# Decay attention: three waits for one count of folded weights become five waits, and the folding is split over the first steps

## The chip, the cores and the metric

The kernel runs on one core of one Trainium2 chip. The metric is the device time of one execution in microseconds, the median over several runs. A profile is one further execution, recorded by the hardware profiler. TensorE is called PE below, its weight loads PEld, VectorE DVE, ScalarE ACT, GpSimd POOL and SyncE SP.

## The reference

The program is a small language model tower on 128 x 128 tokens with 64 channels: an embedding with gates, an attention, a block with mixture of experts, a decay attention and a selected MLP. The change is in the fourth. Cut to it:

```python
low = conv(x, conv_w) + conv_b                     # 5 causal taps over the sequence
hid = layernorm(low + sqrt_beta**2 * (x - low) + x, ln_w, ln_b)
q, k, v = proj(q_w, q_b), proj(k_w, k_b), proj(v_w, v_b)      # 8 heads of 8
scores = q @ k.T / sqrt(8)
p_ = softmax(where(mask, scores, -1e32)) * mask
dist = sqrt(clip((p_.sum(-1) - cumsum(p_)) * pos, 0))
total_effect = clip(exp(-softplus(gammas) * dist), 1e-5, 1e5)
p = softmax(where(mask, scores * total_effect, -1e32)); p[first row] = 0
out = (p @ v) @ out_w.T + out_b
h = h + out        # x is layernorm(h), h includes the experts' output
```

## The kernel before, in words

The tower is five phases, one after another, each a block with one instruction list per engine, written by hand. A phase ends with a barrier over all engines, after which its semaphores are cleared. The residual H (128 partitions x 128 blocks x 64) stays in SBUF all the time. The phase of experts leaves its rows in DRAM (`back_rows`), and `slot` says where each token's row is.

`phase_decay_attention` works on 32 groups of 4 blocks. A group has 4 steps, one for each pair of heads, so 128 steps, numbered K. Each engine runs one loop over K from -24 to 136, with m = K // 4 and j = K % 4. In step K an engine does what is due for pair K, K-1, K-2 and K-3, and at fixed j something for a group ahead: on POOL four gathers (`d_moe`, one in each step, L1463) for group m+6, the join into H (L1476) for m+5 at j = 2, the mean and the centring (`d_mean`, `d_hc`, L1489, L1491) for m+3 at j = 0, the output bias (`d_cb` added to H, L1497) for m+2 at j = 1, and at j = 2 `d_hn` (L1504) for m+2 and `d_xn` (L1510) for m+3. DVE sums H for the mean (L1942) for m+4 at j = 3 and the squares (`d_ss`, the spread, L1890 and L1895) at j = 1. PE turns `d_xn` and `d_hn` (L1578) at j = 3, filters with the taps (`d_conv`, L1603) and projects with `d_wqk` and `d_wv` at j = 0 to 2 and makes the first scores (L1532) of a pair with `d_hide` as mask. So steps -24 to -1 are a ramp in which one group after another goes through gather, join, layer norm, turn, filter, second norm, turn and projection; scores, exponentials, a scan along the keys on DVE (L1901), the decay (`d_decay`, with the positions `d_posg`, L1452 to L1457) on POOL and the weighting follow from K = 0. Order on an engine is fixed; all that isn't due waits behind what is.

Ahead of the loops the weights are loaded by SP (18 loads, L1440) and folded by DVE: the blend with `sqrt_beta` goes into the taps (`d_conv`, `d_convb`), the layer norm's scale and shift into the projections (`d_wqk`, `d_wv`, `d_bqk`, cut into three bf16 parts in `d_bqk_s`), the value bias through the output weights into `d_cb`, `softplus(gammas)` squared into `d_posg`, and the mask into bf16 `d_hide`. A helper `link` makes each DVE instruction wait for the one before. Constants are set by memsets. Fourteen of these instructions add one to the semaphore `ready`, and POOL, PE, ACT and DVE all wait for 14 ahead of their loops:

```python
READY = 14
pool.wait_ge(ready, READY)        # likewise pe, act and dve
for K in range(FIRST, LAST + 1):
```

## Time and profile before

| | us |
|---|---|
| runs | 2621.09, 2600.0, 2622.05; median 2621.09 |
| profiled execution, its time | 2639.77 |
| profiled execution, its span | 2638.0 |
| busy in the span: PE, DVE, ACT, POOL | 2189.6, 1804.3, 1295.3, 1675.9 |
| mean granted TensorE clock | 0.831 of full speed |
| decay attention, from its first load to the end of the last group | about 1263 to 2450 |

The span is from the first to the last instruction of the profiled execution; about 1.8 us of its time lie outside. A busy share tells how much an engine had to do, and the idle time ahead of a group of instructions, with what released it, tells who waited for whom. Times of single instructions are read in the timeline. The granted clock is 0.50 or 1.00 at any moment (1.2 or 2.4 GHz), so a mean between them tells how long it was at each.

### The profile page before, as it was taken

How to read it: one execution, taken by the hardware profiler on the slowest of the kernel's cores; microseconds unless marked ns; L12 is line 12 of the kernel's file. 1: busy time of each engine (PE TensorE's matmuls, PEld its weight loads, DVE VectorE, ACT ScalarE, POOL GpSimd, SP SyncE). 2: the span in 40 equal slices, each digit the busy share in tenths (PEclk: the TensorE clock that was granted, in tenths of full speed). 3: DMA queues.
4: the chain of work that ended last, by engine and by line, in shares of the span. 5: the costliest groups of instructions: out<-in, count | busy, mean ns of one | idle time of the engine just before them, and what ended most of it. 6: DMA issues, size and time to landing. Idle time of an engine off the chain costs nothing. (4 is left out here: it accounts for less than half of the span.)

```text
span 2638.0 us, 56358 instructions
## 1 busy us (share of the span) xinstructions
PE 2189.6 (83%) x20636; PEld 1661.1 (63%) x20636; DVE 1804.3 (68%) x3575; ACT 1295.3 (49%) x2690; POOL 1675.9 (64%) x1809
## 2 busy tenths in 40 slices
PE   6999859999970589998199889999889988998485
PEld 5988736777750455554067677777667776766374
DVE  4599636777749945554368878888888878876524
ACT  1244315666640234444056666666666666665342
POOL 6366113444420765553389999999999999885261
PEclk9999758999985589999578877788888778875587
DMA  2111000000014045668100000000000000000003
GB/s 47 24 38 40 7 8 14 26 22 26 22 33 2 23 103 145 148 145 120 39 7 6 5 6 6 5 6 5 6 6 6 5 5 5 2 1 1 4 1 64
DMA packets 111567, 78.16 MB, mean 30 GB/s; under 512 B 71533, under 2 KB 92269, under 8 KB 111312
## 3 DMA queue, kind: packets, MB, share of 16 engines
q1 hardware_dynamic: 95248, 48.59, 8.2%
q0 software_dynamic: 16064, 26.17, 5.6%
q8 instruction: 161, 2.64, 0.4%
q14 instruction: 94, 0.77, 0.1%
HBM read 56.03 MB, written 18.68 MB: 28 GB/s over the span
## 5 line engine op out<-in xcount | busy, mean ns | idle before, releaser
L1901 DVE TENSOR_TENSOR_SCAN d_later<-d_cont,d_ex 128x768 f32<-128x768 f32 x128 | 283.3, 2213 | 27.1 <-ACT d_ex L1714 26.8
L1684 ACT ACTIVATE d_pT<-d_T 128x384 f32<-128x384 f32 x256 | 125.5, 490 | 295.7 <-PE d_T L1545 295.4
L1545 PE MATMUL d_T<-ident,d_p 128*128 128x128 f32 x768 | 169.3, 339 | 84.3 <-POOL d_p L1470 76.3
L1452 POOL TENSOR_TENSOR d_decay<-d_later,d_posg 128x768 f32<-128x768 f32 x128 | 232.8, 1819 | 9.5 <-DVE d_later L1901 9.5
L1456 POOL TENSOR_TENSOR d_decay<-d_decay,d_rtot 128x512 f32<-128x512 f32 x128 | 179.0, 1399 | 18.9 <-POOL d_decay L1452 0.9
L1463 POOL DMA_INDIRECT d_moe<-back_rows,slot x128 | 130.8, 1022 | 83.5 <-DVE d_mean L1852 60.1
L1532 PEld LDWEIGHTS d_S<-d_kT,d_qT 16*128 16x128 f32 x2048 | 149.9, 220 | 51.5 <-issue 51.5
L1469 POOL TENSOR_TENSOR d_p<-d_p,d_mx 128x512 f32<-128x512 f32 x128 | 162.7, 1271 | 28.7 <-DVE d_mx L1884 26.9
L1532 PEld LDWEIGHTS d_R<-d_kT,d_qT 16*128 16x128 f32 x2048 | 148.5, 218 | 51.2 <-issue 51.2
L1878 DVE SCALAR_TENSOR_TENSOR d_p<-d_decay,d_R 128x768 f32<-128x768 f32 x128 | 121.5, 950 | 85.6 <-PE d_R L1532 54.3
L1532 PE MATMUL d_S<-d_kT,d_qT 16*128 16x128 f32 (+1 forms) x2048 | 169.1, 313 | 0.0
L1532 PE MATMUL d_R<-d_kT,d_qT 16*128 16x128 f32 (+1 forms) x2048 | 167.5, 310 | 0.0
L1545 PEld LDWEIGHTS d_T<-ident,d_p 128*128 128x128 f32 x768 | 95.2, 164 | 112.2 <-POOL d_p L1470 86.2
L223 POOL DMA_INDIRECT rows<-in_table,idx x128 | 122.0, 953 | 35.6 <-issue 31.3
L1720 ACT ACTIVATE d_decay<-d_decay 128x768 f32<-128x768 f32 x128 | 107.3, 838 | 74.9 <-POOL d_decay L1457 74.9
L1457 POOL TENSOR_TENSOR d_decay<-d_decay,d_rtot 128x256 f32<-128x256 f32 x128 | 141.8, 1108 | 0.0
L1322 DVE TENSOR_TENSOR e_cont<-e_h,e_upto 128x512 f32<-128x512 f32 x91 | 62.9, 692 | 107.4 <-ACT e_upto L1199 107.4
L1603 PE MATMUL d_X<-d_conv,d_xT 128*128 128x128 f32 x640 | 119.9, 370 | 1.5 <-ACT d_xT L1773 1.5
L1603 PEld LDWEIGHTS d_X<-d_conv,d_xT 128*128 128x128 f32 x640 | 118.3, 286 | 2.6 <-ACT d_xT L1773 2.6
L1714 ACT ACTIVATE d_ex<-d_ex 128x768 f32<-128x768 f32 x128 | 107.7, 841 | 9.1 <-DVE d_ex L1870 7.8
L1722 ACT ACTIVATE d_decay<-d_decay 128x768 f32<-128x768 f32 x128 | 107.9, 843 | 4.1
L1724 ACT ACTIVATE d_decay<-d_decay 128x768 f32<-128x768 f32 x128 | 107.9, 843 | 4.1
(400 smaller groups left out, 6118.4 us busy)
## 6 DMA issues: line engine op xcount, KB each, us to landing
e_upto<-in_pair_w SPq DMA_DIRECT2D x55, 288.0 KB
e_cont<-in_pair_w SPq DMA_DIRECT2D x36, 288.0 KB
sent_rows<-moe_rows SPq DMA_DIRECT2D x32, 256.0 KB, 2.8
back_rows<-e_ys SPq DMA_DIRECT2D x91, 64.0 KB
out_h<-g_Y SPq DMA_DIRECT2D x8, 512.0 KB, 4.0
rows<-in_table,idx POOLq DMA_INDIRECT x128
d_moe<-back_rows,slot POOLq DMA_INDIRECT x128, 2.5
e_tie<-sent_rows,e_token POOLq DMA_INDIRECT x62
```

What stands on the lines that cost most here:

```text
L223: pool.indirect_dma_start(rows[u][:, b, :], None, dram["table"], bass.IndirectOffsetOnAxis(ap=idx[u][:, b:b + 1], axis=0))\
L1452: pool.tensor_tensor(decay[d][:], later[u][:, 0:2 * SEG].rearrange("p (e s) -> p e s", e=2), posg[:, h:h + 2, :], ALU.mult).then_inc(U["pl ...
L1456: pool.tensor_tensor(long(decay[d]), long(decay[d]), wide(rtot[u], 1, P), ALU.mult)
L1457: pool.tensor_tensor(short(decay[d]), short(decay[d]), wide(rtot[u], 0, HALF), ALU.mult)\
L1463: pool.indirect_dma_start(moe[n % KEEP_M][:, j, :], None, back_rows, bass.IndirectOffsetOnAxis(ap=slot[:, b:b + 1], axis=0))\
L1469: pool.tensor_tensor(long(p2[w]), long(p2[w]), wide(mx2[u], 1, P), ALU.subtract)
L1532: last = nc.tensor.matmul(bank[:, e, cols], qT[s][r, c, (2 * g + S) * P:(2 * g + S + 1) * P], kT[s][r, c, keys], start=False, stop=(g == 1 ...
L1545: last = nc.tensor.transpose(bT[:, t * P:(t + 1) * P], p2[K % KEEP_P][:, e, t * P:(t + 1) * P], ident[:])
L1603: last = nc.tensor.matmul(X1[:, g * P:(g + 1) * P], xT[:, g, tap:tap + P], conv[:, tap, :], start=(tap == 0), stop=(tap == TAPS - 1))
L1684: nc.scalar.activation(pT[w % KEEP_T][:], bT[:, 0:SEG], ACT.Exp).then_inc(U["pT_kept"], 1)
L1878: nc.vector.scalar_tensor_tensor(p2[w][:], decay[d][:], 1e-5, bR[:, :, 0:SEG], ALU.max, ALU.mult).then_inc(U["weighed"], 1)
L1901: nc.vector.tensor_tensor_scan(later[u][:, 1:1 + 2 * SEG], cont[:], ex[u][:].rearrange("p e s -> p (e s)"), 0.0, ALU.mult, ALU.add)\
```

## The change

The count of 14 stays, but its increments come in another order and each engine waits only for the part that it needs next. `READY` becomes five numbers. POOL waits for nothing ahead of its loop; PE, ACT and DVE wait for 8 (four memsets, the bf16 identity, the ones, the taps, the filter's bias). The projections' fold, with `d_cb`, becomes `fold_projections`, called on DVE at the top of step -11; the positions' and the mask's fold becomes `fold_places`, called at the top of step -6. Waits for 11, 12, 13 and 14 stand at the first use of the parts on PE and POOL. The memsets and the cast of the identity move ahead of DVE's wait for the loads. What is computed is the same.

```diff
-        READY = 14
+        CONV_READY, PROJECT_READY, BIAS_READY, PLACE_READY, SCORE_READY = 8, 11, 12, 13, 14
...
             def _(pool):
-                pool.wait_ge(ready, READY)
...
                         pool.wait_ge(U["scanned"], K)
+                        if K == 1:
+                            pool.wait_ge(ready, PLACE_READY)
...
+                            if n == 0:
+                                pool.wait_ge(ready, BIAS_READY)
                             pool.tensor_tensor(hs, hs, cb[:, None, :].to_broadcast([P, GB, D]), ALU.add)\
...
-                pe.wait_ge(ready, READY)
+                pe.wait_ge(ready, CONV_READY)
...
+                        if K + 1 == 0:
+                            pe.wait_ge(ready, SCORE_READY)
...
+                        if m + 1 == 0:
+                            pe.wait_ge(ready, PROJECT_READY)
...
-                act.wait_ge(ready, READY)
+                act.wait_ge(ready, CONV_READY)
...
             def _(dve):
-                dve.wait_ge(loaded, 16 * LOADS)
...
+                nc.vector.memset(xT[:, :, 0:PADT], 0.0).then_inc(ready, 1)
...
+                dve.wait_ge(loaded, 16 * LOADS)
...
+                link(nc.vector.tensor_tensor(bv[:], X1[:, 0:1], bv[:], ALU.add))
+                nc.vector.tensor_copy(bv_wide[:], bv[:, 0:1].to_broadcast([P, P])).then_inc(carried, 1)
+                dve.wait_ge(ready, CONV_READY)
+
+                def fold_projections():
...
+                def fold_places():
...
                 for K in range(FIRST, LAST + 1):
                     m, j = K // PAIRS, K % PAIRS
+                    if K == -11:
+                        fold_projections()
+                    if K == -6:
+                        fold_places()
```

The two functions hold the removed lines word for word, but that the wait for the second fold on PE now stands ahead of the scaling of `d_wqk`.

The start of POOL's list in this phase, before (d_moe are the gathers, H the residual; a wait's semaphore stands in brackets):

```order
L1442 UNCONDITIONAL_BRANCH [waits barrier_Pool_Activation_PE_DVE_SP_gather]
L1463 DMA d_moe<-back_rows,slot 128x64 [waits d_ready]
L1463 DMA d_moe<-back_rows,slot 128x64 x6
L1476 TENSOR_TENSOR H<-H,d_moe 128x256 [waits d_fetched0]
L1463 DMA d_moe<-back_rows,slot 128x64
```

and of the changed kernel:

```order
L1442 UNCONDITIONAL_BRANCH [waits barrier_Pool_Activation_PE_DVE_SP_gather]
L1464 DMA d_moe<-back_rows,slot 128x64 x7
L1477 TENSOR_TENSOR H<-H,d_moe 128x256 [waits d_fetched0]
L1464 DMA d_moe<-back_rows,slot 128x64
L1464 DMA d_moe<-back_rows,slot 128x64 [waits a_rstd_made0] x3
```

The wait for `d_ready` is gone; the order of the instructions is the same.

DVE's list in the projections' fold, before (d_bqk and d_bqk_s are the query and key bias and its bf16 parts, d_bv the value bias):

```order
L1812 TENSOR_SCALAR d_convb<-d_convb,d_biassum 128x64
L1815 TENSOR_TENSOR d_bqk<-d_X,d_bqk 3x512
L1816 TENSOR_SCALAR d_bqk<-d_bqk 3x256
L1817 CAST d_bqk_h<-d_bqk 3x512
L1818 TENSOR_TENSOR d_bqk_rest<-d_bqk,d_bqk_h 3x512
L1819 CAST d_bqk_m<-d_bqk_rest 3x512
L1820 TENSOR_TENSOR d_bqk_l<-d_bqk_rest,d_bqk_m 3x512
```

and the same place in the changed kernel:

```order
L1831 TENSOR_SCALAR d_convb<-d_convb,d_biassum 128x64
L1834 TENSOR_TENSOR d_bqk<-d_X,d_bqk 3x512
L1835 TENSOR_TENSOR d_bv<-d_X,d_bv 128x1
L1836 COPY d_bv_wide<-d_bv 128x128
L1956 TENSOR_REDUCE d_mean<-H 128x4
L1840 TENSOR_SCALAR d_bqk<-d_bqk 3x256
L1841 CAST d_bqk_h<-d_bqk 3x512
```

The first sum over H (L1956) now stands ahead of the fold, and the twelve instructions from L1840 to L1853 stand ahead of the first spread (L1904).

DVE's list around the first second-norm spread, before:

```order
L1928 TENSOR_TENSOR d_zb<-d_X,d_convb 128x256
L1890 TENSOR_REDUCE d_ss<-d_sq 128x4
L1895 TENSOR_REDUCE d_ss<-d_sq 128x4
L1942 TENSOR_REDUCE d_mean<-H 128x4
L1928 TENSOR_TENSOR d_zb<-d_X,d_convb 128x256
```

and in the changed kernel (d_gam and d_posg are the decay rates and the scaled positions):

```order
L1942 TENSOR_TENSOR d_zb<-d_X,d_convb 128x256
L1904 TENSOR_REDUCE d_ss<-d_sq 128x4
L1909 TENSOR_REDUCE d_ss<-d_sq 128x4
L1858 TENSOR_SCALAR d_gam<-d_gam 128x8
L1859 TENSOR_TENSOR d_gam<-d_gam,d_gab 128x8
L1860 TENSOR_TENSOR d_gam<-d_gam 128x8
L1861 TENSOR_TENSOR d_posg<-d_pos,d_gam 128x3072
L1863 CAST d_hide<-d_hide_f 128x384
L1956 TENSOR_REDUCE d_mean<-H 128x4
L1942 TENSOR_TENSOR d_zb<-d_X,d_convb 128x256
```

The five instructions of the positions and the mask now stand between the two spreads and the sum over H.

## Rows read from the trace of the kernel before

**Rows 1.** Busy time by stage: start:end, length, each engine's busy us, TensorE clock, DMA share, GB/s.
```profile
1263.00:1273.30 10.30, 0.00 (x0) 0.00 (x0) 0.00 (x0) 1.28 (x1) 0.00 (x0) 0.50 0.60 167
1336.00:2256.00 920.00, 833.19 (x9317) 651.92 (x9314) 748.59 (x1307) 577.63 (x1039) 877.75 (x855) 0.82 0.03 5
1336.00:1376.00 40.00, 38.41 (x252) 29.63 (x250) 30.66 (x53) 19.88 (x36) 36.08 (x39) 0.66 0.03 6
1576.00:1616.00 40.00, 37.62 (x398) 29.41 (x398) 31.76 (x57) 23.95 (x43) 38.23 (x40) 0.82 0.03 6
```

**Rows 2.** Waits in 1260 to 1345: us in total, times, longest.
```profile
POOL d_moe L1463 <- DVE d_mean L1852: 60.1, 1, 60.1
```

**Rows 3.** Timeline, first load and first DVE instruction: start, us, engine, line, operation [idle before].
```profile
1263.01 0.35 SPq L1440 DMA_DIRECT2D d_wqk<-in_d_wqk  x1
...
1273.31 0.17 DVE L1794 TENSOR_SCALAR d_gab<-d_gam 128x8 f32<-128x8 f32 x1 [12.94 <-DMA d_diag<-in_ident]
```

**Rows 4.** Timeline of DVE, the folding of the weights.
```profile
1279.12 0.28 DVE L1816 TENSOR_SCALAR d_bqk<-d_bqk 3x256 f32<-3x256 f32 x1
...
1283.59 0.14 DVE L1825 TENSOR_TENSOR d_bv<-d_X,d_bv 128x1 f32<-128x1 f32 x1
...
1283.90 0.48 DVE L1827 TENSOR_SCALAR d_wqk<-d_wqk,d_lnw 128x512 f32<-128x512 f32 x1
...
1285.02 0.16 DVE L1834 TENSOR_SCALAR d_gam<-d_gam 128x8 f32<-128x8 f32 x1
...
1285.61 3.36 DVE L1837 TENSOR_TENSOR d_posg<-d_pos,d_gam 128x3072 f32<-128x3072 f32 x1
...
1293.43 0.06 DVE L1852 MEMSET d_mean<- 128x4 f32 x1
```

**Rows 5.** Timeline of POOL, the ramp.
```profile
1293.80 0.94 POOL L1463 DMA_INDIRECT d_moe<-back_rows,slot  x1 [60.13 <-DVE d_mean L1852]
...
1311.02 0.22 POOL L1489 TENSOR_SCALAR d_mean<-d_mean 128x4 f32<-128x4 f32 x1
...
1314.39 0.73 POOL L1476 TENSOR_TENSOR H<-H,d_moe 128x256 f32<-128x256 f32 x1
1315.07 0.61 POOL L1510 TENSOR_TENSOR d_xn<-d_hc,d_rstd 128x256 f32<-128x256 f32 x1
...
1323.25 0.61 POOL L1504 TENSOR_TENSOR d_hn<-d_zb,d_rstd 128x256 f32<-128x256 f32 x1 [0.37 <-ACT d_rstd L1689]
1323.82 0.61 POOL L1510 TENSOR_TENSOR d_xn<-d_hc,d_rstd 128x256 f32<-128x256 f32 x1
```

**Rows 6.** Timeline of DVE and PE, the ramp.
```profile
1312.49 0.42 DVE L1890 TENSOR_REDUCE d_ss<-d_sq 128x4 f32<-128x256 f32 x1 [8.98 <-ACT d_sq L1706]
...
1322.61 0.41 DVE L1942 TENSOR_REDUCE d_mean<-H 128x4 f32<-128x256 f32 x1
...
1324.49 0.69 PE L1578 MATMUL d_X<-ident,d_xn 128*128 128x128 f32 x2 [3.16 <-POOL d_xn L1510]
```

**Rows 7.** Timeline where POOL starts beside a DVE instruction, and one alone.
```profile
1791.20 1.76 DVE L1901 TENSOR_TENSOR_SCAN d_later<-d_cont,d_ex 128x768 f32<-128x768 f32 x1 [0.29 <-ACT d_ex L1714]
...
1791.37 2.43 POOL L1463 DMA_INDIRECT d_moe<-back_rows,slot  x1 [0.15 <-issue]
...
2461.76 1.22 DVE L2155 SCALAR_TENSOR_TENSOR g_X<-g_sums,H 128x1024 f32<-128x1024 f32 x1
2461.78 1.78 POOL L2034 TENSOR_TENSOR g_xw<-g_X,g_wr 128x256 f32<-128x256 f32 x1
...
2464.90 0.72 POOL L2034 TENSOR_TENSOR g_xw<-g_X,g_wr 128x256 f32<-128x256 f32 x1
```

**Rows 8.** Timeline of POOL, d_decay at the start of three groups.
```profile
1513.23 1.83 POOL L1452 TENSOR_TENSOR d_decay<-d_later,d_posg 128x768 f32<-128x768 f32 x1
...
1548.22 1.83 POOL L1452 TENSOR_TENSOR d_decay<-d_later,d_posg 128x768 f32<-128x768 f32 x1
...
1582.24 1.85 POOL L1452 TENSOR_TENSOR d_decay<-d_later,d_posg 128x768 f32<-128x768 f32 x1
```

More of the change, by code:

```diff
@@ L1791, in link @@
                     dve.wait_ge(chain, steps[0])
+                nc.vector.memset(xT[:, :, 0:PADT], 0.0).then_inc(ready, 1)
+                nc.vector.memset(rstd[:], 0.0).then_inc(ready, 1)
+                nc.vector.memset(rstd2[:], 0.0).then_inc(ready, 1)
+                nc.vector.memset(mean[:], 0.0).then_inc(ready, 1)
+                nc.vector.tensor_copy(ident_b[:], ident[:]).then_inc(ready, 1)
+                nc.vector.memset(ones[:], 1.0).then_inc(ready, 1)
+                for u in range(2):
+                    nc.vector.memset(later[u][:, 0:1], 0.0).then_inc(chain, 1)
+                for u in range(KEEP_V):
+                    nc.vector.memset(v[u][:, :, :, HD:HD + 1], 1.0).then_inc(chain, 1)
+                    nc.vector.memset(v[u][:, :, :, HD + 1:], 0.0).then_inc(chain, 1)
+                steps[0] += 2 + 2 * KEEP_V
+                dve.wait_ge(chain, steps[0])
+                dve.wait_ge(loaded, 16 * LOADS)
                 nc.vector.tensor_scalar(gab[:], gam[:], -1.0, None, ALU.mult).then_inc(softened, 1)
@@ L1842, in _ @@
-                for u in range(2):
-                    nc.vector.memset(later[u][:, 0:1], 0.0).then_inc(chain, 1)
-                for u in range(KEEP_V):
-                    nc.vector.memset(v[u][:, :, :, HD:HD + 1], 1.0).then_inc(chain, 1)
-                    nc.vector.memset(v[u][:, :, :, HD + 1:], 0.0).then_inc(chain, 1)
-                steps[0] += 2 + 2 * KEEP_V
-                dve.wait_ge(chain, steps[0])
-                nc.vector.memset(xT[:, :, 0:PADT], 0.0).then_inc(ready, 1)
-                nc.vector.memset(rstd[:], 0.0).then_inc(ready, 1)
@@ L1851, in _ @@
-                nc.vector.memset(rstd2[:], 0.0).then_inc(ready, 1)
-                nc.vector.memset(mean[:], 0.0).then_inc(ready, 1)
-                dve.wait_ge(ready, READY)
+                dve.wait_ge(ready, CONV_READY)
+                def fold_projections():
+                    link(nc.vector.tensor_scalar(bqk[:, 0:2 * P], bqk[:, 0:2 * P], HD ** -0.5, None, ALU.mult))
+                    link(nc.vector.tensor_copy(bqk_h[:], bqk[:]))
+                    link(nc.vector.tensor_tensor(bqk_rest[:], bqk[:], bqk_h[:], ALU.subtract))
+                    link(nc.vector.tensor_copy(bqk_m[:], bqk_rest[:]))
+                    link(nc.vector.tensor_tensor(bqk_l[:], bqk_rest[:], bqk_m[:], ALU.subtract))
+                    link(nc.vector.tensor_scalar(bias[:], bqk_h[:], ident[0:3, 0:1], None, ALU.mult))
+                    link(nc.vector.scalar_tensor_tensor(bias[:], bqk_m[:], ident[0:3, 1:2], bias[:], ALU.mult, ALU.add))
+                    nc.vector.scalar_tensor_tensor(bias[:], bqk_l[:], ident[0:3, 2:3], bias[:], ALU.mult, ALU.add)\
+                        .then_inc(ready, 1)
+                    dve.wait_ge(folded, 2)
+                    link(nc.vector.tensor_scalar(wqk[:], wqk[:], lnw[:, 0:1], None, ALU.mult))
+                    nc.vector.tensor_scalar(wqk[:, 0:2 * P], wqk[:, 0:2 * P], HD ** -0.5, None, ALU.mult).then_inc(ready, 1)
+                    nc.vector.tensor_scalar(wv[:], wv[:], lnw[:, 0:1], None, ALU.mult).then_inc(ready, 1)
+                    nc.vector.scalar_tensor_tensor(cb[:], bT[:, 0:D], notfirst[:, 0:1], outb[:], ALU.mult, ALU.add)\
+                        .then_inc(ready, 1)
@@ new lines, in fold_places @@
+                def fold_places():
+                    dve.wait_ge(softened, 4)
+                    link(nc.vector.tensor_scalar(gam[:], gam[:], 0.0, None, ALU.max))
+                    link(nc.vector.tensor_tensor(gam[:], gam[:], gab[:], ALU.add))
+                    link(nc.vector.tensor_tensor(gam[:], gam[:], gam[:], ALU.mult))
+                    nc.vector.tensor_tensor(posg[:], pos[:, None, :].to_broadcast([P, NH, SEG]), over(gam[:], SEG), ALU.mult)\
+                        .then_inc(ready, 1)
+                    nc.vector.tensor_copy(hide[:], hide_f[:]).then_inc(ready, 1)
```

24 lines of the change are left out of this document (removed).

## The prediction

> **What bounds the kernel now.** I read the busy time by stage first, then the longest waits around the start of the decay attention, then the timeline of each engine there. The stage has two parts. Once it runs, POOL is its bound: busy 877.75 of 920 us, 95%, where PE has 833.19 and DVE 748.59 [rows 1]. But before it runs there is a long hole: POOL waits 60.1 us, in one piece, for DVE's last memset [rows 2]. The loads of the stage are issued from 1263.01 and DVE's first instruction starts at 1273.31 [rows 3]; DVE then folds weights until 1293.43 [rows 4], and POOL's first gather of the expert rows starts at 1293.80 [rows 5]. Nothing of the stage runs beside this: all engines wait for one count of 14. After it a ramp (gather, join, layer norm, turn, filter, second norm, projection) leads to the first scores, and the POOL-bound flow follows. As each engine goes through its list in order, what the ramp starts earlier ends earlier, unless something new is late in it.
>
> **The wait removed, on POOL.** POOL now waits for nothing of the stage before the first gather. It follows the same barrier as the loads of 1263.01, and 1293.80 came 0.3 us after the memset that released it, so the first gather starts near 1263.3, 30.5 us earlier. Its own work from the first gather to the first mean (d_mean, 1311.02) took 17.2 us [rows 5]: 1280.5. From there to the end of the third join (1314.39 + 0.73) it is 4.1 us: 1284.6.
>
> **The prologue that stays, on DVE.** Memsets and the cast of the identity now stand ahead of the wait for the loads and are hidden by them (10.3 us without DVE work). The chain on the filter taps is unchanged and starts at 1273.31. The instruction at 1279.12 [rows 4] is the first that moves out; the bias and its wide copy come in (about 0.4 us, the distance 1283.59 to 1283.90 and one start more), so DVE enters its loop at about 1279.6. The first sum over H takes 0.4: 1280.0. That is just ahead of POOL's 1280.5, so neither waits long.
>
> **The first part moved, K = -11.** The projection fold stands on DVE between the first sum and the first spread. It is 1279.12 to 1283.59 and 1283.90 to 1285.02 [rows 4], 4.5 + 1.1 = 5.6 us: DVE gets to the spread at 1285.6. The squares for it are there by 1282.0 (the spread followed d_mean by 1312.49 - 1311.02 = 1.5 us [rows 5, 6]), so 3.6 us of waiting are new here. From the spread to a possible start of d_hn or d_xn are the 0.42 of the sum and two small activations, about 1 us (the next time round d_hn at 1323.25 followed 0.64 us behind the start of the instruction after such a spread [rows 5, 6]), so the first d_xn starts at 1286.6 where POOL would be free at 1284.6: 2.0 us of the 30.5 are given back, and the chain at this point runs through the loads, DVE's prologue and this fold. First gain: 1315.07 - 1286.6 = 28.5 us.
>
> **What the overlap costs there.** Before, POOL stood still while DVE folded; now both work. The trace shows what DVE and POOL do to each other: a gather that starts under a scan of DVE takes 2.43 us instead of 0.94, a POOL tensor_tensor under a scalar_tensor_tensor of DVE takes 1.78 instead of 0.72 [rows 5, 7]. Both are DVE instructions with two operands in SBUF. DVE in turn waits for a running POOL instruction. In 1280 to 1285.6 POOL wants to run d_mean 0.22, d_hc (as d_xn) 0.61 and a join 0.73, 1.56 us; and a join stands beside the tap chain (0.73). Bounds: nothing, or 2.3 us. The nearest rows are these collisions, so I take 1.5, plus 0.3 us for the 18 loads, since eight gathers of 32 KB join 1.7 MB there at a DMA share of 0.60 [rows 1] (bounds 0 and 1.6 us, 256 KB at the 167 GB/s shown). POOL's own delay by DVE, up to 0.7 us for each of some 10 gathers and joins, is free as long as it stays under 2 + 1.8 us. Gain at the first d_xn: 28.5 - 1.8 = 26.7 us.
>
> The trace of before has no row in which POOL runs beside a DVE instruction with a single SBUF source. The Trainium skill, page "SBUF — State Buffer", section "SBUF: two separate sides", says that such instructions, in their two-port mode (an fp32 copy is its example), shut GpSimd out too, and that a gather issued by GpSimd then waits for its descriptors. That speaks against this change: eight gathers and more now stand beside tensor_scalars, casts and copies. By it POOL would use up its slack, and the sum would be at the second rival's time; no row here shows it.
>
> **The second part moved, K = -6.** The positions fold (d_gam, then d_posg 3.36 us, then d_hide) stands on DVE after two spreads and ahead of a sum over H. In time of before, d_posg would start 0.59 us (1285.02 to 1285.61 [rows 4]) after 1322.61 [rows 6], at 1323.20. POOL starts d_hn at 1323.25 and d_xn at 1323.82 [rows 5]. d_posg has two SBUF operands like the scan and the instruction of rows 7, so I count that it keeps POOL out for its whole length: whichever comes first, d_xn ends 3.3 us later. And d_xn is what PE waits for: it turns it at 1324.49 [rows 6], and filter, projections and first scores hang on that. The sum over H behind d_posg comes about 4 us later than 1322.61, but POOL asks for it only after this d_xn, two gathers and two copies, which are late by the same 3.3 us: hidden. Bounds 0 and 3.7 us; I take 3.3, from the nearest rows. d_cb, the bias weights and d_hide are done long before POOL, PE or the scores ask for them, at K = -7, -4 and -1; those new waits cost nothing.
>
> **Sum.** 30.5 - 2.0 - 1.8 - 3.3 = 23.4 us, which no later stage gives back by its order, since POOL has the same list. The profiled execution took 2639.77 us (span 2638.0), 18.7 above the median of the runs, 2621.09. Against its own time the sum gives 2616.4; against the median 2597.7.
>
> **Rivals.**
> First: d_posg doesn't hold POOL (no row shows a plain tensor_tensor of this length beside POOL), and the mutual waits are small. Then 26.7 to 28.5 us stay: 2594.4 to 2592.6, just over 1%. For it: POOL runs unhindered beside all DVE instructions that read PSUM. Against: both instructions of rows 7.
>
> Second: the prologue's gathers or their landing become the path. With 15 gathers ahead of the first d_xn, and 10 of them under DVE's work, 0.7 us each (half of the 1.49 of rows 5 and 7) is 7 us: POOL ends the third join at 1291.6, d_xn is 3.2 us later than my 1288.4, and the gain 20 us: 2601. With 1.4 us each it would be 13 us: 2608. Loads that come late through the gathers' share of the queues act in the same direction, one for one.
>
> Third, in the flow: the distance of every fourth d_decay was 35.0 us (1513.23 to 1548.22) and then 34.0 (1548.22 to 1582.24) [rows 8], by how DVE's scans fall against POOL's instructions. A start in another position could hold one of them: half a microsecond in each of the 26 groups that 920 us hold is 13 us, in either direction. I put that in the range.
>
> Fourth, slower: TensorE's clock. In 1336 to 1376 the granted clock was 0.66, PE was busy 38.41 of 40 us and POOL only 36.08; at 0.82 POOL had 38.23 [rows 1]. If the changed start led to the low clock all through the stage, PE would be the bound: 920 x (38.23 / 36.08 - 1) = 55 us more, minus 23 is 32 slower: 2653. It decides where the mean clock of the stage falls to about 0.7, from 0.82. Against: the clock was at 0.50 ahead of this stage before, too [rows 1], and most of POOL's idle time in that window is the ramp itself.
>
> **How the numbers follow.** Forecast 0.49, first rival 0.19, second 0.21, third in its harmful form 0.06, fourth 0.05. The likeliest gives 2597.7 us. The runs of before lie between 2600.0 and 2622.05, so 1% (26 us) is also about what a measurement tells from no change. The lowest end takes the first rival or the useful form of the third, 2597.7 less 24: 2574; the highest leaves a third of the second rival and of the harmful third above it, 2612. Faster by over 1% needs 26.2 us: the first rival, and one part in three of the forecast with the third's useful half, 0.35. Slower by over 1% is the fourth, 0.05. The rest, 0.60, is within 1%.
>
> **What would show it.** Right: a first gather at 1263 to 1264; the first sum over H near 1280; the first spread 5.6 to 7 us behind it with POOL waiting for the reciprocal deviation; a d_hn or d_xn of about 3.9 us beside d_posg; that d_xn 22 to 25 us before its 1323.82; POOL busy 95% after. Wrong: gathers of 1.5 us and more in the prologue, loads that end after 1275, no long d_xn beside d_posg, or an unchanged start of the flow.

## The result, and the profile after

The changed kernel takes 2597.51 us in the median of 20 runs (2580.04 to 2641.18); the kernel before, run beside it, 2620.0 us (2600.0 to 2656.05, 20 runs). The ratio is 0.9914, with a 95% interval of 0.989 to 0.9938: about 22.5 us less, between 16 and 29. The ratios here and below, with their intervals, are taken over the fast runs alone, those within 1.5% of the fastest of the same kernel. The profiled execution has a span of 2600.9 us where the one of before had 2638.0. These two spans differ by 37.1 us, more than the runs do, and the first thing to read is how little of that is the change.

I take the trace apart at two points that every profile of this kernel has: the issue of the decay attention's first load, and the first table load of the last phase (the selected MLP) on ACT. Ahead of the first point the two programs are the same, and behind the second too.

| us | before | changed |
|---|---|---|
| phases ahead, to the first load | 1263.01 | 1242.84 |
| first load to the first scores | 72.56 | 45.43 |
| first scores to the last phase | 1112.73 | 1112.57 |
| last phase | 189.70 | 200.06 |
| span | 2638.0 | 2600.9 |

So 37.1 = 20.2 + 27.1 + 0.2 - 10.4. Only the 27.1 belongs to the change; the 20.2 and the 10.4 are chance, as the experiments below show. All times from here on that are called "after the first load" are counted from the first row of the table.

The busy time by stage of the changed kernel (start:end, length, PE, PEld, DVE, ACT, POOL busy, clock, DMA share, GB/s): the loads, then a 920 us stretch of the flow like that of [rows 1], then the middle of the last phase.

```profile
1242.90:1253.20 10.30, 0.00 (x0) 0.00 (x0) 3.79 (x14) 1.23 (x1) 7.71 (x9) 0.50 0.69 189
1315.70:2235.70 920.00, 834.20 (x9453) 652.94 (x9451) 741.66 (x1311) 583.69 (x1049) 876.26 (x853) 0.82 0.02 5
...
2434.50:2506.50 72.00, 68.92 (x402) 55.50 (x404) 16.36 (x43) 28.31 (x53) 51.85 (x79) 0.70 0.00 1
```

Where [rows 1] had DVE and POOL at 0.00 while the loads ran, they now have 3.79 and 7.71. In the flow nothing changed: POOL 876.26 of 920 against 877.75, clock 0.82. In the last row PE is busy 68.92 of 72 us at a clock of 0.70. The same stretch of the kernel before is this:

```profile
2482.00:2554.00 72.00, 60.69 (x425) 49.08 (x425) 19.39 (x50) 30.01 (x56) 58.84 (x89) 0.83 0.00 1
```

More matmuls (425 against 402) in the same 72 us with less busy time, at 0.83. At 0.70 PE is busy 96% of the stretch, at 0.83 84%: the longer last phase goes with the lower clock.

The longest waits around the start of the phase in the changed kernel (us in total, times, longest; 1240 to 1325):

```profile
POOL d_moe L1464 <- POOLq L91: 31.6, 1, 31.6
...
PE d_X L1581 <- POOL d_xn L1513: 10.7, 2, 7.5
...
DVE d_zb L1942 <- PE d_X L1606: 8.9, 2, 6.3
```

POOL's 60.1 us for the last memset [rows 2] became 31.6, and what releases it is its own queue passing the barrier. Nothing of that wait is left in this phase. Next come waits of 6 to 8 us of PE for POOL and of DVE for PE: the ramp waits for itself now, one engine for the next.

The timeline of the changed kernel in the prologue and ramp, all engines (start, us, engine, line, operation [idle before]):

```profile
1242.84 0.35 SPq L1440 DMA_DIRECT2D d_wqk<-in_d_wqk  x1
...
1243.48 0.94 POOL L1464 DMA_INDIRECT d_moe<-back_rows,slot  x1 [31.62 <-POOLq L91]
...
1254.00 0.17 DVE L1813 TENSOR_SCALAR d_gab<-d_gam 128x8 f32<-128x8 f32 x1 [6.82 <-DMA d_diag<-in_ident]
...
1255.33 1.42 POOL L1464 DMA_INDIRECT d_moe<-back_rows,slot  x1 [0.30 <-issue]
...
1258.01 1.39 POOL L1477 TENSOR_TENSOR H<-H,d_moe 128x256 f32<-128x256 f32 x1
...
1260.41 0.41 DVE L1956 TENSOR_REDUCE d_mean<-H 128x4 f32<-128x256 f32 x1
1260.74 0.27 DVE L1840 TENSOR_SCALAR d_bqk<-d_bqk 3x256 f32<-3x256 f32 x1
...
1261.90 0.37 POOL L1490 TENSOR_SCALAR d_mean<-d_mean 128x4 f32<-128x4 f32 x1
...
1262.66 0.98 DVE L1844 TENSOR_TENSOR d_bqk_l<-d_bqk_rest,d_bqk_m 3x512 bf16<-3x512 f32 x1
...
1267.07 0.40 DVE L1904 TENSOR_REDUCE d_ss<-d_sq 128x4 f32<-128x256 f32 x1
...
1268.03 0.61 POOL L1513 TENSOR_TENSOR d_xn<-d_hc,d_rstd 128x256 f32<-128x256 f32 x1 [1.42 <-ACT d_rstd L1696]
...
1276.01 0.61 POOL L1507 TENSOR_TENSOR d_hn<-d_zb,d_rstd 128x256 f32<-128x256 f32 x1 [0.18 <-ACT d_rstd L1696]
...
1276.10 0.54 DVE L1860 TENSOR_TENSOR d_gam<-d_gam 128x8 f32<-128x8 f32 x1
1276.58 0.61 POOL L1513 TENSOR_TENSOR d_xn<-d_hc,d_rstd 128x256 f32<-128x256 f32 x1
1276.68 3.73 DVE L1861 TENSOR_TENSOR d_posg<-d_pos,d_gam 128x3072 f32<-128x3072 f32 x1
...
1277.34 3.93 POOL L1464 DMA_INDIRECT d_moe<-back_rows,slot  x1
...
1288.25 0.61 POOL L1507 TENSOR_TENSOR d_hn<-d_zb,d_rstd 128x256 f32<-128x256 f32 x1 [0.24 <-ACT d_rstd L1696]
1288.27 1.11 PE L1535 MATMUL d_S<-d_kT,d_qT 16*128 16x128 f32 x16
```

The reader should see four things. The first gather starts 0.64 us after the first load. The first sum over H starts as soon as DVE's prologue ends (1260.41), and the fold between it and the spread (1260.74 to 1267.07) is what POOL waits 1.42 us for in front of the first d_xn. The second d_xn (1276.58) starts 0.10 us ahead of d_posg (1276.68) and takes its normal 0.61; the gather behind it is the one that d_posg holds, 3.93 us instead of 0.99. And the d_hn of the next group (1288.25) has waited 0.24 us for its reciprocal deviation. The timeline of the kernel before, at the same two instructions:

```profile
1335.55 0.61 POOL L1504 TENSOR_TENSOR d_hn<-d_zb,d_rstd 128x256 f32<-128x256 f32 x1 [3.26 <-ACT d_rstd L1689]
1335.57 1.11 PE L1532 MATMUL d_S<-d_kT,d_qT 16*128 16x128 f32 x16
```

It waited 3.26 us. The three microseconds that the gather lost to d_posg were three that POOL would have stood idle a little later.

### The profile page after: what moved, and what is told of

It is laid out like the page before. It is cut to its first block and busy times, and to the rows that moved or that the text cites. A ratio compares the mean times of both kernels' runs of the same rounds, so it can differ in the third digit from the quotient of the medians.

```text
span 2600.9 us, 56361 instructions
## 1 busy us (share of the span) xinstructions
PE 2181.0 (84%) x20636; PEld 1652.0 (64%) x20636; DVE 1799.9 (69%) x3575; ACT 1294.4 (50%) x2690; POOL 1682.9 (65%) x1809
## 5 line engine op out<-in xcount | busy, mean ns | idle before, releaser
L1915 DVE TENSOR_TENSOR_SCAN d_later<-d_cont,d_ex 128x768 f32<-128x768 f32 x128 | 277.1, 2165 | 32.0 <-ACT d_ex L1721 31.8
L1470 POOL TENSOR_TENSOR d_p<-d_p,d_mx 128x512 f32<-128x512 f32 x128 | 158.9, 1242 | 28.7 <-DVE d_mx L1898 26.9
L1464 POOL DMA_INDIRECT d_moe<-back_rows,slot x128 | 141.4, 1105 | 55.0 <-POOLq L91 31.6
L1606 PE MATMUL d_X<-d_conv,d_xT 128*128 128x128 f32 x640 | 113.4, 356 | 1.5 <-ACT d_xT L1780 1.5
L1606 PEld LDWEIGHTS d_X<-d_conv,d_xT 128*128 128x128 f32 x640 | 111.1, 271 | 2.6 <-ACT d_xT L1780 2.6
```

What stands on the lines that cost most here:

```text
L1464: pool.indirect_dma_start(moe[n % KEEP_M][:, j, :], None, back_rows, bass.IndirectOffsetOnAxis(ap=slot[:, b:b + 1], axis=0))\
L1470: pool.tensor_tensor(long(p2[w]), long(p2[w]), wide(mx2[u], 1, P), ALU.subtract)
L1606: last = nc.tensor.matmul(X1[:, g * P:(g + 1) * P], xT[:, g, tap:tap + P], conv[:, tap, :], start=(tap == 0), stop=(tap == TAPS - 1))
L1915: nc.vector.tensor_tensor_scan(later[u][:, 1:1 + 2 * SEG], cont[:], ex[u][:].rearrange("p e s -> p (e s)"), 0.0, ALU.mult, ALU.add)\
```

## The experiments

Theory A is that of the prediction: the gain is the head start of POOL's list minus what ends last in the ramp, each microsecond of the ramp reaches the end of the flow one for one, and d_posg keeps POOL out for its length, so that it costs 3.3 us when it starts ahead of a d_hn or d_xn and nothing when it holds a gather. The rivals are that d_posg doesn't matter, that the loads or the flow's position decide, or that the 22.5 us have more to do with chance than with the ramp; each expectation says which it is about. For each run the places read are the same. Times are after the first load but for the last two columns, the first load itself and the span; the first column is empty where DVE starts on four loads instead of 18.

| us | first DVE work | first d_xn | second d_xn | first scores | scores to last phase | last phase | first load at | span |
|---|---|---|---|---|---|---|---|---|
| before | 10.30 | 52.06 | 60.81 | 72.56 | 1112.73 | 189.70 | 1263.01 | 2638.0 |
| changed | 11.16 | 25.19 | 33.74 | 45.43 | 1112.57 | 200.06 | 1242.84 | 2600.9 |
| changed, again | 10.70 | 24.72 | 33.21 | 44.83 | 1109.10 | 200.03 | 1234.94 | 2588.9 |
| changed, third | 10.76 | 24.70 | 33.10 | 44.70 | 1109.10 | 189.58 | 1223.82 | 2567.2 |
| d_posg first | 11.22 | 25.80 | 37.26 | 49.37 | 1113.01 | 189.61 | 1278.61 | 2630.6 |
| fold one step later | 11.01 | 22.83 | 35.63 | 46.42 | 1111.52 | 189.60 | 1256.16 | 2603.7 |
| gathers wait for loads | 10.30 | 32.95 | 45.14 | 56.21 | 1108.29 | 189.67 | 1231.53 | 2585.7 |
| before, POOL's wait removed | 11.09 | 36.16 | 44.50 | 55.99 | 1112.28 | 189.74 | 1267.59 | 2625.6 |
| d_posg from one source | 11.07 | 24.87 | 33.23 | 44.81 | 1109.07 | 189.62 | 1238.40 | 2581.9 |
| taps first | | 22.50 | 32.83 | 43.81 | 1108.29 | 189.61 | 1237.39 | 2579.1 |
| short ramp | | 19.98 | 30.34 | 41.81 | 1112.31 | 189.62 | 1230.36 | 2574.1 |
| taps first, fold two steps later | | 22.92 | 31.74 | 43.33 | 1109.03 | 189.66 | 1235.98 | 2578.0 |

**The changed kernel again.** No edit.

> The changed kernel once more, unchanged. In its profile the last phase took 200.1 us against 189.7 before, with the same instructions, and PE's granted clock in its middle was 0.71 against 0.83; the phases ahead of the decay attention took 20 us less. Theory A (both are the clock's chance, not the change): the time from the phase's first load to the last phase is again 1158 us within 1, while the last phase and the first part take other values. Theory B (the shifted start puts the last phase into a low clock): the last phase takes 200 us again.

It took 2590.72 us. The ramp repeats within 0.6 us (first scores 44.83). Theory A missed in its number all the same: from the first load to the last phase it was 1153.9 us, not 1158 within 1, since the flow came out 3.5 us shorter. And the last phase was 200.03 again, as theory B has it, so the same program ran a third time:

> The changed kernel a third time, unaltered. Both of its profiles so far show a last phase of 200.0 us where the eight other kernels' profiles show 189.6 to 189.7. If that is tied to this kernel's text, it will be 200.0 again; if it is chance (a state of TensorE's clock in that phase), 189.6 is about as likely. Either way the ramp must repeat: d_xn of the second group near 33.2 to 33.7 us after the phase's first load, first scores near 44.8 to 45.4, last phase's start near 1153.9 or 1158.0 after the first load.

It took 2569.01 us, the ramp repeated again (44.70), and the last phase was 189.58, with PE at the clock of the kernel before in the same stretch of that phase:

```profile
2411.30:2483.30 72.00, 60.81 (x425) 49.22 (x425) 19.32 (x50) 29.91 (x55) 58.80 (x89) 0.83 0.00 1
```

So the long last phase isn't tied to the text of the changed kernel. Three profiles of one program differ by 19.0 us (1242.84 against 1223.82) ahead of the first load, by 3.5 us in the flow, and by 10.5 us in the last phase, and by 0.7 us in the ramp. A single span says little about this change; the ramp shows it to within 0.7 us.

**d_posg in front of d_hn.** The three d_gam instructions move from the positions' fold to the end of the projections' fold, so that d_posg starts right behind the spread.

```diff
-
-                def fold_places():
                     dve.wait_ge(softened, 4)
                     link(nc.vector.tensor_scalar(gam[:], gam[:], 0.0, None, ALU.max))
                     link(nc.vector.tensor_tensor(gam[:], gam[:], gab[:], ALU.add))
                     link(nc.vector.tensor_tensor(gam[:], gam[:], gam[:], ALU.mult))
+
+                def fold_places():
                     nc.vector.tensor_tensor(posg[:], pos[:, None, :].to_broadcast([P, NH, SEG]), over(gam[:], SEG), ALU.mult)\
```

The wait for `softened` moves with them.

> The changed kernel with the three small d_gam instructions moved from step -6 to the end of the projections' fold, so that in step -6 d_posg stands first and can start about 1.4 us earlier, before d_hn and d_xn of POOL. Theory A (d_posg costs nothing in the changed kernel only because it starts 0.1 us behind the second d_xn and then holds up a gather instead, whose delay PE doesn't see): now d_hn or d_xn is held for about 3.3 us, the second d_xn comes 36.5 to 37.5 us after the phase's first load instead of 33.7, the first scores 48 to 49 us instead of 45.4. Theory B (d_posg doesn't hold a POOL tensor_tensor, or the ramp has slack for it): the second d_xn stays at 33.7 or, by the fold's three instructions, within 0.6 us of it, and the first scores at 45.4 to 46.

Measured 2632.37 us in one run, with the phase's first load at 1278.61, the latest of all. The timeline of POOL and DVE there:

```profile
1311.91 3.52 DVE L1861 TENSOR_TENSOR d_posg<-d_pos,d_gam 128x3072 f32<-128x3072 f32 x1
...
1312.55 3.35 POOL L1507 TENSOR_TENSOR d_hn<-d_zb,d_rstd 128x256 f32<-128x256 f32 x1 [0.34 <-ACT d_rstd L1696]
1315.87 0.72 POOL L1513 TENSOR_TENSOR d_xn<-d_hc,d_rstd 128x256 f32<-128x256 f32 x1
```

d_hn took 3.35 us instead of 0.61 and ended 0.47 us behind d_posg. The second d_xn is at 37.26 instead of 33.1 to 33.7 and the first scores at 49.37 instead of 44.7 to 45.4, 3.9 to 4.7 us later and beyond the 48 to 49 of theory A. Part of that isn't the collision: the first d_xn is already 0.6 to 1.1 us late, with the three d_gam instructions now in the fold ahead of it. From the first d_xn to the second it is 11.5 us instead of 8.4 to 8.6, about 3 us, near the 3.3 of the prediction. In the changed kernel d_posg started 0.10 us behind the start of the second d_xn, in its two repeats 0.10 and 0.67 us. That d_posg doesn't hold POOL (the first rival) is refuted.

**d_posg from one source.** Eight tensor_scalars, one for each head, in the place of the one tensor_tensor.

```diff
-                    nc.vector.tensor_tensor(posg[:], pos[:, None, :].to_broadcast([P, NH, SEG]), over(gam[:], SEG), ALU.mult)\
+                    for g in range(NH - 1):
+                        nc.vector.tensor_scalar(posg[:, g, :], pos[:], gam[:, g:g + 1], None, ALU.mult).then_inc(chain, 1)
...
+                    nc.vector.tensor_scalar(posg[:, NH - 1, :], pos[:], gam[:, NH - 1:NH], None, ALU.mult).then_inc(ready, 1)
```

> The changed kernel with d_posg made by eight tensor_scalar instructions of 128 x 384 (one SBUF source and one scalar per partition, so one operand stream) instead of one tensor_tensor with two. Theory A (only DVE instructions with two SBUF operands keep POOL out): POOL's gather behind the second d_xn takes its 0.99 us instead of 3.93. Theory B (fp32 instructions with one SBUF source keep it out too, one instruction at a time): the gather starts in a gap between two of them or waits for one, and takes 1.0 to 1.6 us; POOL instructions behind it are lengthened by up to 0.4 us each. In both the fold is some 0.3 us longer or shorter, and the first scores stay at 44.8 to 45.4.

Measured 2583.66 us in one run. Timeline of DVE and POOL:

```profile
1272.30 2.69 DVE L1862 TENSOR_SCALAR d_posg<-d_pos,d_gam 128x384 f32<-128x384 f32 x7
...
1272.39 0.99 POOL L1464 DMA_INDIRECT d_moe<-back_rows,slot  x1
1273.68 1.00 POOL L1464 DMA_INDIRECT d_moe<-back_rows,slot  x1 [0.30 <-issue]
...
1276.23 0.23 POOL L1490 TENSOR_SCALAR d_mean<-d_mean 128x4 f32<-128x4 f32 x1 [0.64 <-DVE d_mean L1959]
```

Neither gather is held (0.99 and 1.00 us), which was the number of theory A. But POOL's next two instructions are, by a little, which was theory B (timeline of POOL):

```profile
1274.69 0.55 POOL L1483 COPY d_hTr<-d_hT 128x256 f32<-128x256 f32 x1
1275.20 0.40 POOL L1484 COPY d_hTr<-d_hT 128x128 f32<-128x128 f32 x1
```

Beside no tensor_scalar, in the changed kernel, they take 0.40 and 0.28 us. And the edit changed two things at once, the number of SBUF operands and the length of each instruction, 0.40 us in the place of 3.36: what starts beside so short a one can be held only for its rest. So this run doesn't show that it is the two operands that hold POOL. Other rows show that one is enough, as here in the timeline of DVE and POOL of the next experiment:

```profile
1256.96 0.47 DVE L1851 TENSOR_SCALAR d_wqk<-d_wqk,d_lnw 128x512 f32<-128x512 f32 x1
...
1257.09 0.92 POOL L1478 TENSOR_TENSOR H<-H,d_moe 128x256 f32<-128x256 f32 x1
```

The join that starts 0.13 us behind this tensor_scalar takes 0.92 us instead of 0.73. A d_hc that starts 0.14 us into the cast d_bqk_m takes 0.74 to 0.75 instead of 0.61 in five profiles. Sums are the exception: no join beside the spread (d_ss) takes more than 0.74.

For two operands, the Trainium skill, page "SBUF — State Buffer", section "SBUF: two separate sides", says that a DVE instruction with two SBUF inputs holds the pair of ports that it shares with GpSimd against a GpSimd instruction that reads SBUF; the traces here agree (3.35 us for d_hn beside d_posg), with gathers held too. The first scores are at 44.81, where two of the three profiles of the changed kernel have 44.70 and 44.83: a gather freed there is worth nothing, since POOL then stands idle 2.21 us ahead of its next d_hn.

**Gathers wait for the loads.** POOL waits for the 18 loads ahead of its loop, and DVE's prologue and fold stay as changed.

```diff
             def _(pool):
+                pool.wait_ge(loaded, 16 * LOADS)
                 for K in range(FIRST, LAST + 1):
```

> The changed kernel with POOL waiting for the 18 loads ahead of its first gather. Theory A (the loads end 0.86 us later than before because eight gathers share the DMA queues with them, and POOL's 15 gathers ahead of the first d_xn are nearly the critical path): DVE's first instruction is back at 10.3 us after the first load, the first gather comes at 10.6, the first d_mean at about 28 to 29 and the first d_xn at 32 to 33 instead of 25.2, so the first scores at 52 to 53. Theory B (the loads' end varies by itself): DVE's first instruction stays near 11.2.

Measured 2587.48 us in one run. First scores at 56.21, 10.8 to 11.5 us later than in the changed kernel. Without gathers beside them the loads end at 10.30 after the first, exactly as in the kernel before; with them, in the other rows of the table, at 10.70 to 11.22. What I had not foreseen is 3.2 to 4.2 us on top of the expected 52 to 53: with POOL's list elsewhere against DVE's, d_posg met d_hn again (timeline of DVE and POOL):

```profile
1272.88 3.36 DVE L1862 TENSOR_TENSOR d_posg<-d_pos,d_gam 128x3072 f32<-128x3072 f32 x1
...
1272.92 3.79 POOL L1508 TENSOR_TENSOR d_hn<-d_zb,d_rstd 128x256 f32<-128x256 f32 x1 [0.62 <-ACT d_rstd L1697]
```

So the collision is not avoided by the changed kernel's order of instructions alone. Here POOL stood idle 0.62 us ahead of d_hn, and DVE's three d_gam instructions (0.16 to 0.17 us each) and the start of d_posg fit in. In the three profiles of the changed kernel POOL was idle 0.04 to 0.18 us there, and its join, d_hn and d_xn, one right behind the other, held d_gam back until d_xn had started. In the third profile all three were held (0.64, 0.60 and 0.53 us), and d_posg came when d_xn was over (timeline of POOL and DVE):

```profile
1256.92 0.61 POOL L1513 TENSOR_TENSOR d_xn<-d_hc,d_rstd 128x256 f32<-128x256 f32 x1
...
1257.59 3.36 DVE L1861 TENSOR_TENSOR d_posg<-d_pos,d_gam 128x3072 f32<-128x3072 f32 x1
```

It depends on tenths of a microsecond of POOL's idle time, which nothing in the kernel ties down.

**Only POOL's wait removed.** The kernel before, without the one line; the whole fold stays in DVE's prologue.

```diff
             def _(pool):
-                pool.wait_ge(ready, READY)
                 for K in range(FIRST, LAST + 1):
```

> The kernel before with POOL's wait for the 14 removed alone; PE, ACT and DVE keep theirs, and all folding stays ahead of DVE's loop. Theory A (two halves of the gain: POOL's early start, and DVE's early loop): POOL runs its gathers and stops at its first d_mean, DVE enters its loop about 31 us after the first load as before, the first d_xn comes about 3 us later, at 34 to 36 us instead of 52.1 (before) and 25.2 (changed), the first scores at 54.5 to 56.5, a gain of 16 to 18 us of the 27. Theory B (gathers alone bound the ramp): nearly the whole 27 us. Theory C (DVE's order alone): no gain.

Measured 2627.36 us in one run. The first d_xn is at 36.16, just past the expected 34 to 36; the first scores are at 55.99, 16.6 us earlier than before, of the 27.1 that the whole change wins. The bound has passed to DVE, as POOL's timeline shows:

```profile
1299.72 0.22 POOL L1488 TENSOR_SCALAR d_mean<-d_mean 128x4 f32<-128x4 f32 x1 [13.40 <-DVE d_mean L1941]
```

POOL, ready early, waits 13.40 us for the first sum over H, which stands behind the whole fold. Clearing DVE's prologue is worth the other 10.6 us: the two folds that moved into the ramp, and the memsets and the cast that moved under the loads. No run separates these; in the kernel before the memsets and the cast took 4.3 of the 20.2 us of the prologue.

**The projections' fold one step later.** It moves behind the first spread.

```diff
-                    if K == -11:
+                    if K == -10:
                         fold_projections()
```

> The changed kernel with the projections' fold called in step -10 instead of -11, so behind the first spread and its sum on DVE. Theory A (the fold ahead of the spread is what gives back about 2 us of the early start, and DVE has 6 us of idle time behind the spread to hide it): the spread comes 19.5 to 21 us after the first load instead of 24.2, the first d_xn then waits for POOL's third join alone and comes at 22.5 to 24 instead of 25.2, and the first scores at 43 to 44.3 instead of 44.8 to 45.4. Theory B (POOL's gathers and joins bound this place anyway): the spread is early, but the first d_xn and the first scores stay within 0.5 us.

Measured 2605.46 us in one run. The first d_xn is 1.9 to 2.4 us earlier (22.83), as the term of 2.0 in the prediction has it, but the second is 1.9 to 2.5 us later and the first scores are at 46.42, 1.0 to 1.7 later than in the changed kernel. A miss, and POOL's timeline says why:

```profile
1284.09 0.22 POOL L1490 TENSOR_SCALAR d_mean<-d_mean 128x4 f32<-128x4 f32 x1 [2.07 <-DVE d_mean L1956]
...
1288.09 3.06 POOL L1477 TENSOR_TENSOR H<-H,d_moe 128x256 f32<-128x256 f32 x1
1291.11 0.72 POOL L1507 TENSOR_TENSOR d_hn<-d_zb,d_rstd 128x256 f32<-128x256 f32 x1
```

The fold now stands ahead of the second sum, and POOL's second mean waits 2.07 us for it: what was won is lost one step on. POOL's next join starts at 31.9 after the first load, as in the changed kernel (31.8 to 32.3). But d_posg comes 2.3 to 2.8 us sooner, at 31.0 instead of 33.3 to 33.8, since PE had its first d_xn sooner, and catches the join in front of d_hn: 3.06 us instead of 0.73.

**Taps first, and d_posg tied down.** Three things: from the last run the fold at step -10; the four loads of the filter taps first and with a semaphore of their own, so that the tap chain starts before the other fourteen, in a new order, have landed; and d_posg behind POOL's second d_xn by a wait.

```diff
+                for dst, name in ((beta, "d_beta"), (conv, "d_conv"), (convb, "d_convb"), (diag, "ident")):
+                    sp.dma_start(dst[:], dram[name]).then_inc(taps_loaded, 16)
...
+                dve.wait_ge(taps_loaded, 64)
...
+                    dve.wait_ge(G["xn_made"], 2)
                     nc.vector.tensor_tensor(posg[:], pos[:, None, :].to_broadcast([P, NH, SEG]), over(gam[:], SEG), ALU.mult)\
```

> The variant with the fold in step -10, and besides: the four loads of the taps' folding come first, with a semaphore of their own, and DVE folds the taps while the others land; d_posg waits for the second d_xn of POOL. Theory A (loads, then DVE's prologue, set the time of the first sum over H): DVE enters its loop at about 11.5 to 12.5 us instead of 17.1 to 17.6, POOL's 13 gathers and two joins bound the first mean at 18 to 19, and the first scores come at 42 to 43. Theory B (DVE's prologue was hidden by POOL's gathers already): no more than with the fold's move alone.

Measured 2580.89 us in one run; first scores at 43.81, 0.9 to 1.6 us earlier than in the changed kernel, and short of the expected 42 to 43. DVE's first sum over H starts at 15.9 after the first load, not at 11.5 to 12.5: the rest of its prologue still waits for the other loads and for PE. POOL's first mean is at 18.35, as expected. d_posg waits for d_xn and holds a gather again (timeline of DVE and POOL):

```profile
1270.94 3.36 DVE L1866 TENSOR_TENSOR d_posg<-d_pos,d_gam 128x3072 f32<-128x3072 f32 x1 [2.67 <-POOL d_xn L1516]
...
1271.01 4.17 POOL L1467 DMA_INDIRECT d_moe<-back_rows,slot  x1 [0.16 <-issue]
```

The wait kept d_posg off the join and d_hn, but the held gather took up all of POOL's slack: ahead of its next d_hn POOL was not idle at all. What the wait alone is worth no run shows. POOL's second mean still waits 2.08 us for the sum behind the fold. One run more moved the fold behind that sum:

```diff
-                    if K == -10:
+                    if K == -8:
                         fold_projections()
```

> Taps loaded first as in the kernel before it in this study, and the projections' fold at step -8 instead of -10: behind the second sum over H, ahead of the first d_zb. The second mean on POOL should no longer wait (its 2.08 us go), but the fold, 6 to 7 us from about 23.5 after the first load, now ends about 2.3 us after PE's filter result is there, so the first d_zb is late by that. Theory A (what ends last in the ramp is the chain through the first d_zb and d_hn): first scores 0 to 2 us later than the 43.81 of the version with the fold at -10. Rival (POOL's list with the second mean is what ends last): first scores up to 2 us earlier, near 42.

Measured 2579.79 us in one run. The second d_xn comes 1.1 us earlier (31.74 for 32.83), the first scores 0.5 (43.33). The 2.08 us are gone, and the feared delay of d_zb is not there, since PE's filter result was late itself. Timeline of DVE in this run:

```profile
1265.11 0.42 DVE L1947 TENSOR_TENSOR d_zb<-d_X,d_convb 128x256 f32<-128x256 f32 x1 [1.44 <-PE d_X L1609]
...
1266.64 1.74 DVE L1863 TENSOR_TENSOR d_gam<-d_gam,d_gab 128x8 f32<-128x8 f32 x1
```

DVE was idle 1.44 us ahead of d_zb, waiting for PE. Neither theory had the whole: POOL's list gained 1.1 us, and less than half of that reached the scores. TensorE's clock took the rest. Behind the second d_xn PE does the same 20 filter matmuls in every version; they took 4.64 us here, at a granted clock of 0.50, and 4.02 us in the taps-first run, where the clock rose on the way (0.59 in the mean). In the twelve profiles these 20 take 3.85 us (the fold one step later) to 4.64 us, and 4.63 to 4.64 before and in all three profiles of the changed kernel. So the 27.1 us stand, and differences of under a microsecond between the first scores of versions do not: by the second d_xn, which comes ahead of these matmuls, taps first wins 0.3 to 0.9 us over the changed kernel and the fold two steps later 1.4 to 2.0.

**A shorter ramp.** On top of the taps-first version (with the fold at step -10): gathers five groups ahead instead of six, joins four instead of five, and the loop starts at -20. Nine gathers instead of thirteen stand ahead of the first mean.

```diff
-        FIRST, LAST = -24, NQ + 8
+        FIRST, LAST = -20, NQ + 8
...
-                    n = m + 6
+                    n = m + 5
                     if there(n):
                         b = n * GB + j
...
-                    n = m + 5
+                    n = m + 4
                     if j == 2 and there(n):
```

> The variant above with the ramp four steps shorter: gathers for group m+5 and joins for m+4 instead of m+6 and m+5, loops from step -20, so that 9 gathers instead of 13 stand ahead of the first mean. Theory A (POOL's gathers then bound the ramp): the first mean at 13 to 14 us, the first scores at 37.5 to 39, the whole 33 to 35 us faster than the kernel before where the other phases agree. The steady flow keeps its 34.4 us per group, since POOL does the same work, unless DVE's sum over H now waits for a join that stands one group nearer; theory B: that wait appears and the flow gets slower by up to 1 us per group, 30 us in all, so that nothing is won.

Measured 2583.04 us in the median of 6 runs (2575.86 to 2622.02) where the kernel before beside it has 2613.38 (13 runs): 0.9892, 95% interval 0.9869 to 0.9915. The first scores are at 41.81, 2.9 to 3.6 us earlier than in the changed kernel, and the flow behind them isn't longer than others (1112.31), so theory B is refuted. Theory A missed as well: the first mean is at 15.8, not 13 to 14, and the scores are short of 37.5 to 39. POOL now waits in the prologue, in its timeline:

```profile
1246.20 0.23 POOL L1493 TENSOR_SCALAR d_mean<-d_mean 128x4 f32<-128x4 f32 x1 [3.06 <-DVE d_mean L1961]
```

With fewer gathers ahead of it, it waits for DVE's first sum over H, so DVE's prologue bounds the start and not the gathers.

The timed gain is larger than the changed kernel's 0.9914 by its middle, but the intervals overlap (0.989 to 0.9938), and the two were timed in different batches. That it beats the changed kernel is what its ramp shows, three microseconds of it; the times alone don't show it.

## Why the prediction was right, point by point

The median came out at 2597.51 us, forecast 2597.7. That closeness is luck: the sum was 23.4 us, the ramp's measured gain is 27.1, and the runs, whose interval is 16 to 29, can't tell the two apart. The terms up to the first d_xn came out; the last, 3.3 us, measured nothing. By the prediction's own signs, no long d_xn beside d_posg was one of being wrong, and the second d_xn came 27.1 us earlier, not 22 to 25.

- **POOL's wait, 30.5 us.** The first gather starts 0.64 after the first load, before 30.79 [rows 3, 5]: 30.15 us. Right.
- **The prologue that stays on DVE, to the first sum over H.** By the forecast it starts at 1279.6 in time of before, 16.6 after the first load; measured 17.57. The loads end 0.86 us late with the gathers beside them (0.40 and 0.46 in the two other profiles), for which 0.3 was in the sum with bounds of 0 and 1.6. Within the bounds, too small.
- **The fold ahead of the spread, 2.0 us given back.** Forecast 5.6 us without waits; measured 6.33 (1260.74 to 1267.07), with 0.98 where 0.68 is usual for d_bqk_l and 0.69 where 0.29 is usual for the second scaling of d_wqk. POOL waited 1.42 us behind it, as the prediction said it would. Taking the fold away from this place gave 1.9 to 2.4 us at the first d_xn (the fold one step later). Right.
- **Mutual waits, 1.8 us with the loads.** DVE's path: 0.86 of loads, 0.27 in the tap chain and its neighbours (6.08 us from the first instruction to d_bv where rows 3 and 4 leave 5.81 to the same place), 0.7 in the fold: 1.9 us. POOL was 1.6 us behind the forecast at the first mean (19.06 for 17.5), by one gather of 1.42, one join of 1.39 and small pieces, and this was covered by the wait for the fold, as the prediction had it. Gain at the first d_xn 52.06 - 25.19 = 26.9, forecast 26.7. Right.
- **d_posg holds d_hn or d_xn, 3.3 us. This is the step that failed.** Not by its mechanism: d_posg holds POOL for its whole length (3.35 and 3.79 us on d_hn in two experiments, 3.06 on a join in a third, 2.99 to 4.17 on gathers that start behind it). It failed by the start. The prediction let d_posg start 0.59 us behind the spread, from [rows 4]; but there POOL had stood still. With POOL at work, the first and third of d_gam's three instructions were themselves held, by POOL's join and d_hn (0.49, 0.17 and 0.54 us), it was 1.31 us from the first of them to d_posg (1275.37 to 1276.68), and d_xn had started 0.10 us before. "Whichever comes first, d_xn ends 3.3 us later" overlooked the third case, that both have started first. The gather behind them was held instead, and POOL's later idle 3.26 us took that up. Measured on the path: 0.
- **No later stage gives it back.** First scores 27.1 us earlier, last phase 27.3 us earlier after the first load (1185.29 and 1158.00). Right, and in the two other profiles too, with 3.5 us more by the flow's chance.

The rivals: the first had the right number (26.7 to 28.5) for a wrong reason. The second (gathers become the path) didn't come: of the four gathers that start beside DVE's prologue (1254.00 to 1260.41) one took 1.42 us, the others 0.94 to 0.96, and beside the fold none took more than 1.28. Of the third, a flow that depends on its start, there are two lengths, 1108.3 to 1109.1 and 1111.5 to 1113.0 us, 3.5 apart rather than 13; since the same program shows both, they aren't the change's doing. The fourth, the clock: 0.82 in the flow as before. The slow clock did appear elsewhere, in the last phase, at 10.4 us.

The sentence of the Trainium skill that the prediction set against the change (page "SBUF — State Buffer", section "SBUF: two separate sides": a DVE instruction with one source, in its two-port mode, shuts GpSimd out too) has its rows after all, and they agree with it. The trace doesn't name the mode, but the tensor_scalar and the cast above have one source in SBUF and held a join and a d_hc, and a gather that starts 0.17 to 0.19 us into the cast d_bqk_h takes 1.05 to 1.07 us instead of 0.94 in four profiles. The gain did not suffer as the second rival had it, since these instructions are short: none held POOL for more than 0.2 us. The prediction was also wrong that the trace of before has no row beside a single source: the sum over H at 1303.09 (0.42 us) has a gather beside it from 1303.14 that takes 0.95.

## What to carry to other kernels

One count for all of a prologue's results is a barrier that nobody wrote down: give each part its own threshold (four waits for 14 became seven waits at five counts here), and then look for the engine that was behind the barrier next to the one you freed (here POOL alone was worth 16.6 of 27.1 us, DVE's prologue the rest). When the fold moves into the ramp, ask of each long DVE instruction what POOL starts beside it, and of each chain of short ones what on POOL can hold it back: the same 3.4 us cost nothing beside a gather with idle time behind it, and 3 to 4 beside a norm that PE waits for. Cut the trace at points that both programs share before comparing spans.

## What the runs showed of the hardware that I had not expected

- DVE is held by POOL as well, and small instructions show it best: a cast of 3 x 512 that takes 0.41 us took 1.68 beside a join and a d_xn (the fold one step later), and with the fold two steps later a tensor_tensor of 128 x 8 took 1.74 instead of 0.17 beside a join, d_hn and d_xn (1266.64 in its timeline above). DVE's sums over SBUF were never held: all 384 sums over H in the twelve profiles took 0.39 to 0.42 us, and all 768 spreads 0.40 to 0.42.
- What holds a gather: a tensor_tensor of 3.36 us (up to 4.17 instead of 0.99) and in the prologue the 128 x 640 product of the taps (1.42). Eight tensor_scalars of 128 x 384, 0.40 us each, did not (0.99 and 1.00). Of the memsets of d_v the runs show nothing: they overlap gathers of 0.94 us, but no gather starts inside one.
- It matters which of the two starts first. Two gathers that started 0.10 us ahead of d_posg took their normal 0.97 and 0.99 us beside it, and d_posg its 3.36.
- The last phase has two lengths, 189.6 to 189.7 us in ten profiles and 200.0 in two, with a granted clock of 0.83 or 0.70 over the same 72 us and 425 or 402 matmuls in them. Both came from one program. What tips it stays open.
- The phases ahead of the changed place, the same text in all twelve profiles, took from 1223.8 to 1278.6 us. A single run therefore says nothing about a change of 1%.
